# A two-layer graph kernel: the transposes of h move from TensorE to the DMA queue

## The reference, cut to what matters

```python
x = _layernorm(x + _L0_gnn_ref(x, wq, wk, adj, bm), axis=-1)         # this is h
x = _layernorm(x + _L1_gnn_ref(x, adj, W_lang, W_grav, W_V, W_O, gate_logit, log_sigma), axis=-1)

# inside _L1_gnn_ref, with h = x:
z_l = h @ W_lang.T;  z_g = h @ W_grav.T;  v = h @ W_V.T
A_l = relu(zn @ zn.T) * not_eye          # zn: the normed rows of z_l
A_g = exp(-d2(z_g) / (2 sigma**2)) * not_eye
K = w_l * rows(A_l * adj) + (1 - w_l) * rows(A_g * adj)
out = (K @ v) @ W_O.T
```

## Time and profile before

| | before |
|---|---|
| median of 3 runs | 1203.28 us (1202.04 to 1203.45) |
| the profiled execution, its own time | 1203.25 us |
| its span | 1201.2 us |
| one full step | 70.32 us |
| PE, DVE, ACT, POOL busy in the full step from 497.01 us | 65.48, 57.92, 40.67, 20.89 us |
| PE busy over the span | 90% |
| DVE busy over the span | 79% |

### The profile page before, as it was taken

The page is one execution under the profiler, slowest core; times in us unless marked ns, Lnnn a source line. Parts: engine busy times, 40 slices in busy tenths (PEclk is TensorE's granted clock), DMA queues, the critical chain, the costliest instruction groups (busy, mean ns, idle before and its releaser), DMA issues.

```text
span 1201.2 us, 20240 instructions
## 1 busy us (share of the span) xinstructions
PE 1077.6 (90%) x7296; PEld 709.7 (59%) x7296; DVE 948.7 (79%) x2678; ACT 657.8 (55%) x1299; POOL 332.6 (28%) x316
## 2 busy tenths in 40 slices
PE   7667999989999898999989998989989998998996
PEld 4344756756565575656557565656756575675653
DVE  4456878978787897878789787878978787897867
ACT  2445547565564756556465655656565565656531
POOL 0131413233041323304132230413223041322200
PEclk9979999999999999999999999999999999999998
DMA  7002003020110202002020200202020020201000
GB/s 263 0 1 71 1 1 106 1 106 1 40 67 1 106 1 106 1 33 74 1 106 1 106 1 30 77 1 106 2 97 9 25 82 1 106 1 71 1 36 35
DMA packets 22836, 56.35 MB, mean 47 GB/s; under 512 B 1744, under 2 KB 2256, under 8 KB 20688
## 3 DMA queue, kind: packets, MB, share of 16 engines
q1 hardware_dynamic: 22736, 55.06, 12.7%
HBM read 21.50 MB, written 16.78 MB: 32 GB/s over the span
## 4 chain that ended last, share of the span: by engine, by line
DVE 30%; PE 29%; issue 18%; ACT 15%; POOL 6%; DMA 1%; SPq 0%; DVEq 0%; POOLq 0%; ACTq 0%
PE bank L224 8%; PE bank L226 8%; PE bank L225 8%; DVE att L825 5%; DVE a_g L925 4%; POOL att_lo L1102 4%; DVE o_stat L747 3%; DVE z_lo L832 3%; ACT vb L509 2%; ACT a_g L534 2%; ACT att_hi L515 2%; PE bank L412 2%; ACT z_hi L549 2%; PE bank L462 2%; ACT b_row L522 2%
## 5 line engine op out<-in xcount | busy, mean ns | idle before, releaser
L1102 POOL TENSOR_TENSOR att_lo<-att,att_hi 128x512 f16<-128x512 f32 x128 | 154.8, 1217 | 176.0 <-ACT att_hi L515 160.0
L825 DVE SCALAR_TENSOR_TENSOR att<-a_row,u_col,vb 128x512 f32<-128x512 f32 x128 | 130.4, 1038 | 41.0 <-POOL att_lo L1102 39.5
L224 PE MATMUL bank<-xw_hi,att_hi 128*128 128x257 f16 x512 | 141.7, 277 | 15.6 <-DVE ug_lo L703 14.6
L224 PE MATMUL bank<-ht_hi,z_hi 128*128 128x256 f16 x512 | 139.6, 273 | 4.9 <-issue 3.9
L226 PE MATMUL bank<-xw_hi,att_lo 128*128 128x257 f16 x512 | 140.8, 275 | 0.0
L225 PE MATMUL bank<-xw_lo,att_hi 128*128 128x257 f16 x512 | 140.5, 274 | 0.0
L226 PE MATMUL bank<-ht_hi,z_lo 128*128 128x256 f16 x512 | 139.6, 273 | 0.0
L225 PE MATMUL bank<-ht_lo,z_hi 128*128 128x256 f16 x512 | 139.6, 273 | 0.0
L515 ACT ACTIVATE att_hi<-att 128x512 f16<-128x512 f32 x128 | 79.8, 623 | 52.7 <-DVE att L825 52.7
L582 ACT ACTIVATE agg_t<-bank,den_inv 128x256 f32<-128x256 f32 x128 | 58.9, 473 | 89.7 <-DVE den_inv L772 89.7
L603 ACT ACTIVATE xw_hi<-bank 128x256 f16<-128x256 f32 x128 | 48.9, 384 | 107.8 <-PE bank L226 107.8
(11 more groups left out here) (177 smaller groups left out, 2801.0 us busy)
## 6 DMA issues: line engine op xcount, KB each, us to landing
x_in<-in_x SPq DMA_DIRECT2D x16, 1024.0 KB, 5.4
x_res<-x_in SPq DMA_DIRECT2D x16, 1024.0 KB, 5.3
out_y<-o SPq DMA_DIRECT2D x32, 512.0 KB, 3.3
agg_t<-in_wl SPq DMA_DIRECT2D x4, 256.0 KB, 3.8
y<-in_wg SPq DMA_DIRECT2D x1, 1024.0 KB, 9.8
o<-in_wv SPq DMA_DIRECT2D x1, 1024.0 KB, 11.9
h<-in_woT SPq DMA_DIRECT2D x1, 1024.0 KB, 14.1
att<-in_adjT SPq DMA_DIRECT2D x1, 256.0 KB, 4.1
```

The source lines that it names most:

```text
L224: pe.matmul(dst, ah, bh, start=(i == 0 and first), stop=False, skip_group_check=skip)
L825: dve.scalar_tensor_tensor(out=att[:, g % 2, :], in0=a_row[:, j, :], scalar=u_col[:, j, n:n + 1], in1=vb[:, g % 2, :], op0=ALU.mult, op1=A ...
L1102: pool.tensor_tensor(att_lo[:, n[0], n[1], :], att[:, g % 2, :], att_hi[:, n[0], n[1], :], ALU.subtract).then_inc(s["att_lo_done"], 1)
```

## The change

h is split before it is transposed. ACT rounds each tile of h to `h_hi`, DVE subtracts to `h_lo`, both in SBUF, and SP's queue issues eight DMA transposes, a `hi` and a `lo` one for each tile, that write `ht_hi` and `ht_lo` directly. TensorE's 16 transposes are gone, the eight x products of the next pair stand in one piece, and the first z product of the next step waits for all eight transfers. On DVE and ACT the tiles of h and of xw alternate.

```diff
+        h_hi, h_lo = sb("h_hi", [2 * OC, N], F16), sb("h_lo", [2 * OC, N], F16)
...
+                if l0:
+                    wait(sp, s["v_mm"], 4 * q)
+                    for k in range(4):
+                        cols = slice(k * P, (k + 1) * P)
+                        sp.wait_ge(s["h_hi_done"], 4 * q + k + 1)
+                        sp.dma_start_transpose(ht_hi[:, :, cols], h_hi[:, k, :]).then_inc(s["ht_hi_landed"], 16)
+                        sp.wait_ge(s["h_lo_done"], 4 * q + k + 1)
+                        sp.dma_start_transpose(ht_lo[:, :, cols], h_lo[:, k, :]).then_inc(s["ht_lo_landed"], 16)
...
-                        if g == 0 and not up:
-                            pe.wait_ge(s["ht_lo_done"], 4 * p + 4)
-                        if g < 4 and up:
-                            pe.wait_ge(s["ht_lo_done"], 4 * p + g + 1)
+                        if g == 0:
+                            pe.wait_ge(s["ht_hi_landed"], 64 * p + 64)
+                            pe.wait_ge(s["ht_lo_landed"], 64 * p + 64)
...
-                    for k in range(8 if x_first else 4):
-                        wx_product(k)
-                if l0:
-
-                    pe.wait_ge(s["h_done"], 4 * q + 4)
-                    for d in range(DC):
-                        for k in range(4):
-                            last = pe.transpose(bank[d][:, k * P:(k + 1) * P], h[:, k, d * P:(d + 1) * P], ident[:])
-                        last.then_inc(s["ht_mm"], 1)
-                if new and not at(p, -2, -1):
-                    for k in range(4, 8):
+                    for k in range(8):
                         wx_product(k)
...
+                def h_hi_tile(k):
+                    act.wait_ge(s["h_done"], 4 * q + k + 1)
+                    wait(act, s["ht_hi_landed"], 64 * q)
+                    act.activation(h_hi[:, k, :], h[:, k, :], ACT.Copy).then_inc(s["h_hi_done"], 1)
+
-                if new:
-                    for k in range(8 if at(p, -1) else 4):
+                if at(p, -1):
+                    for k in range(8):
                         xw_hi_tile(k)
-                if l0:
-                    for d in range(DC):
-                        act.wait_ge(s["ht_mm"], 4 * q + d + 1)
-                        act.activation(ht_hi[:, d, :], bank[d][:], ACT.Copy).then_inc(s["ht_hi_done"], 1)
+                for k in range(4):
+                    if l0:
+                        h_hi_tile(k)
+                    if new and not at(p, -1):
+                        xw_hi_tile(k)
...
+                def h_lo_tile(k):
+                    dve.wait_ge(s["h_hi_done"], 4 * q + k + 1)
+                    wait(dve, s["ht_lo_landed"], 64 * q)
+                    dve.tensor_tensor(h_lo[:, k, :], h[:, k, :], h_hi[:, k, :], ALU.subtract)\
+                       .then_inc(s["h_lo_done"], 1)
+
...
-                    for k in range(4, 8) if x_first else range(4):
+                if x_first:
+                    for k in range(4, 8):
                         xw_lo_tile(k)
-                if l0:
-                    for d in range(DC):
-                        dve.wait_ge(s["ht_hi_done"], 4 * q + d + 1)
-                        dve.tensor_tensor(ht_lo[:, d, :], bank[d][:], ht_hi[:, d, :], ALU.subtract)\
-                           .then_inc(s["ht_lo_done"], 1)
+                for k in range(4):
+                    if l0:
+                        h_lo_tile(k)
+                    if new and not x_first:
+                        xw_lo_tile(k)
```

More of the change, by code:

```diff
@@ L161, in build @@
             att_lo_done ot_mm den_done agg_done to_mm relu_done y_done y_odd_done y_stat_done y_mv_done
-            y_var_done y_rstd_done h_done ht_mm ht_hi_done ht_lo_done z_mm z_hi_done z_lo_done t_mm
+            y_var_done y_rstd_done h_done h_hi_done h_lo_done ht_hi_landed ht_lo_landed z_mm z_hi_done z_lo_done t_mm
             t_hi_done t_lo_done s_mm sq_l_done sq_lc_done r_l_done neg_g_done shift_done diag_r_done
```

## The result

The changed kernel takes 1265.3 us, median of 4 runs (1264.66 to 1267.64), against 1203.37 before: 1.051 times as long, with a 95% interval of 1.049 to 1.054. The prediction was 1255, in a range of 1204 to 1310.

A forecast was written before the change was run, and what follows sets the result against it. A chain through several engines, with PE and DVE arriving together, sets the step. To 1203.28 us it added 32.9 in 14 full steps and 8.1 and 10.9 at the two ends, 51.9 in all: 1255, range 1204 to 1310.

The forecast's parts named there:

- The removed work: 16 PE transposes in each of 16 steps: PE and DVE arrive together, q_part within 0.2 us of before; counted 0.
- The landing: Last ht_lo transpose in a full step: six queue issues of 1.2 us behind h_lo0 at 514.05, then 3.3 us to land.
- T: Time at which the full step's last DMA transpose, lo3, lands: 514.05 + 7.2 + 3.3 = 524.55 us.
- The clock: PE stands over 6 us before the z products, and the lowered granted clock adds 2.0 us on the first of them.
- The full step: z_lo0 starts at 529.95, 2.35 us late, and the attention rows with it; 14 x 2.35 = 32.9 us.
- The ends: Hand-overs to p = 0 and p = 15, where transposes land late: 8.1 and 10.9 us more.
- Only the ends pay: Rival: at 0.47 us an issue, full steps stay at 70.32 and only the first and last hand-overs lose; 1208 to 1212; chance 0.18.
- Each piece is paid for: Rival: each DMA transpose costs 3.4 us, 32 pieces an engine at 107 ns, none overlapping; 1480 us; chance 0.08.
- Faster: Rival: h_lo far under 0.61 us shrinks DVE's stretch to q_part with PE's, 1.75 us a step; 1183 us; chance 0.06.

The follow-up runs named there:

- run in one piece with q_part first: Against the kernel before: eight x products in one piece, TensorE's 16 transposes behind them, xw_lo and q_part ahead of ht_lo on DVE; 1182.95 us, 0.983.
- the `hi` first: Against the changed kernel: the same eight DMA transposes, issued hi0 to hi3 and then lo0 to lo3; 1243.76 us, 1.035 times before.
- with pairs: Against the changed kernel: h_hi and h_lo of a tile side by side, one 128 x 1024 DMA transpose for both, four issues a step; 1223.8 us, 1.016 times before.
- with a ninth: Against the changed kernel: one more DMA transpose a step, h_lo0 again into a tile that nothing reads; 1293.53 us, 28 us more than the change.
- run with PE kept busy: Against the changed kernel: 24 idle matmuls in each full step, 56 at the ends, ahead of the wait for the landings; 1236.47 us, 1.028 times before.
- paired kernel with PE kept busy: Against the kernel with one 128 x 1024 transpose a tile: 12 idle matmuls in each full step, 44 at the ends; 1216.23 us, 1.011 times before.

## Why the prediction was right

**The removed work is worth nothing in the full steps.** Right: q_part stands 9.11 us behind h after, 9.06 before. The run in one piece with q_part first says the same from the other side, since the transposes are still on PE there and the kernel is 20 us faster than before. No run takes the transposes away and leaves the order of the rest as it was.

**The landing.** Right in sum, in part by luck: T was put 11.16 us behind the start of h_lo0 (524.55 less 513.39). In the step shown the last transpose lands 11.03 us behind it (545.68 less 534.65) and the z products start at 11.17. Two of its terms were off and cancelled: the issues follow every 1.30 us and not every 1.2, which makes 0.6 in six of them, and the landing takes 2.5 and not 3.3. That the queue holds it, in strict order, is shown by the runs with the `hi` first, with pairs and with a ninth.

**The clock.** Right in mechanism and, on average, in size. The sum had 5.4 us from the landing to z_lo0, of which 2.0 were chosen for the clock between 1.4 and 2.6; on average of 13 hand-overs z_lo0 starts 5.43 us behind the z products (4.71 to 5.95). The run with PE kept busy shows that it costs: it took 1.75 us off the step.

**The full step.** It lost 3.14 us rather than 2.35, 0.8 more. By the means of the traces, 0.24 of it is the landing, which longer issues delay in some hand-overs; 0.14 is that in the step of the rows z_lo0 stood later before (17.36 us behind h) than on average (17.22); 0.28 arose between z_lo0 and a_row, where the prediction had DVE without a gap and DVE stood for the second z_hi; the remaining 0.13 lies mostly behind a_row.

**The ends.** To p = 0 the interval grew by 8.1 us, as forecast, but the attention rows were 8.6 late and 0.6 was won back behind them. To p = 15 it is the tail's 14.8 less a full step's 3.1, 11.6 against 10.9: the z products start 8.9 us later, as forecast, and 11 matmuls at the lower clock behind a wait of 13.2 us cost 2.3 rather than 2.0; the other 0.4 was not traced. With 11 us too little in the full steps, 0.7 in the last one, and 2.1 us of setup on the other side, 1255 became 1265.

**The rivals.** *Only the ends pay* had its point of decision at an issue of 0.81 us; it fell with 1.30. The paired kernel with PE kept busy comes near to it, at 1216. *Each piece is paid for* fell too: 69632 packets more (92368 less 22736) with a share of 19.0% of 1262.8 us for all, against 12.7% of 1201.2, is 1398 engine-us, 20 ns a packet and not 107. *Faster* would have needed a shorter h_lo; h_lo takes 0.69 us, and 0.60 until the next instruction starts.

The 261 GB/s that the Trainium skill has for such transfers (DMA: Bandwidth & Descriptors, Latency and other measured facts) would make 0.5 us for 128 KB, an estimate. Here a second 128 KB in the same issue added 0.8 us to the landing; either is small beside the issues. The 1309 ns of the Trainium skill's VectorE: DVE Perf Modes, The three transpose paths, for one 128 x 128 block are near the 1264 that an issue takes here with four blocks in it; taken as a price by the block it would be four times too high. The measurement decides.

## What to carry to other kernels

At the two sizes measured here, 128 x 512 and 128 x 1024, a DMA transpose was paid for in the issuing queue by the instruction: put more in one, and order the queue by when the data is ready. Before work is moved off the busiest engine, ask whether a second engine arrives at the same moment. Here two orders on DVE, with the same 256 transposes on TensorE, were 35 us apart (1183 and 1218), and taking the 256 away did not bring q_part forward. A wait of 6 us put on TensorE in place of work cost twice, once as the wait and once as the slower matmuls behind it, and matmuls whose result nobody reads took most of the second part away.

## What was not expected of the hardware

Issuing a DMA transpose holds SP's queue for 1.26 us at 512 columns and 1.32 at 1024, where a plain copy of 1 MB takes 0.47. Single issues take up to 2.54 us. Idle matmuls added to a kernel made it 29 us faster, with the mean granted clock at 0.985 against 0.936. And DVE's tensor_scalar on float32 in SBUF, 0.54 us alone, took twice as long beside a subtraction on POOL (two tiles 2.02 us instead of 1.00).
